# One unit of a fused transformer layer: VectorE's attention products move behind its FFN relu

## The reference

```python
q, k, v = tokens @ Wq + bq, tokens @ Wk + bk, tokens @ Wv + bv     # 16 heads of 64
S = einsum('bthd,buhd->btuh', q, k) - dist_scale * |t - u|          # a few (u, head) masked
P = softmax(S / sqrt(64), axis=u)
x = layernorm(tokens + einsum('btuh,buhd->bthd', P, v) @ Wo + bo)
z = layernorm(relu(x @ W1 + b1) @ W2 + b2 + x)                      # W1: 1024 -> 4096
```

## Time and profile before

| | us |
|---|---|
| median of 3 runs (1418.12 to 1552.58) | 1418.31 |
| the profiled execution, as timed | 1416.82 |
| its span on the slowest core, core 1 | 1415.0 |
| spans of the 8 cores | 1403.4 to 1415.0 |
| PE busy | 1288.8 (91%) |
| ACT busy | 836.9 (59%) |
| DVE busy | 788.6 (56%) |
| ACT L819, 512 exponentials | 521.6 |
| DVE L825, 512 products | 352.2 |
| ACT L1058, 176 relus of the FFN | 98.6 |
| DVE L859, 64 products with reciprocals | 44.1 |

### The profile page before, as it was taken

One profiled execution on the slowest core, in us unless ns is written; L12 is line 12 of the kernel. 1 busy time (PEld: TensorE's weight loads), 2 busy tenths in 40 slices (PEclk: granted clock), 3 DMA queues, 4 the chain that ended last, 5 costly groups with the idle time before them and its releaser, 6 DMA issues.

```text
span 1415.0 us, 20648 instructions; the slowest of 8 cores (1403.4 to 1415.0 us)
## 1 busy us (share of the span) xinstructions
PE 1288.8 (91%) x6612; PEld 618.1 (44%) x6612; DVE 788.6 (56%) x1279; ACT 836.9 (59%) x1177; POOL 37.7 (3%) x67
## 2 busy tenths in 40 slices
PE   3889899999889999999899999989999999889995
PEld 2444344444334644444355444444544444445443
DVE  5865045455468544369584443885834438773146
ACT  4755477777655756767567567674665766613122
POOL 1010100000000000000000000000000000000000
PEclk9999999999999999999999999999999999999999
DMA  9957699999943412216634222165431222677435
GB/s 230 242 162 169 110 123 122 135 120 117 120 142 106 150 58 99 94 49 176 209 103 141 93 94 84 53 186 192 131 123 64 100 91 68 173 244 216 157 89 173
DMA packets 116223, 187.65 MB, mean 133 GB/s; under 512 B 55934, under 2 KB 93828, under 8 KB 105224
## 3 DMA queue, kind: packets, MB, share of 16 engines
q1 hardware_dynamic: 87688, 156.77, 35.8%
q0 software_dynamic: 28416, 29.41, 17.9%
HBM read 178.86 MB, written 45.09 MB: 158 GB/s over the span
## 4 chain that ended last, share of the span: by engine, by line
PE 75%; DVE 9%; ACT 6%; issue 6%; DMA 3%; SPq 0%; DVEq 0%; ACTq 0%
PE PS L243 75%; ACT EB L819 2%; DVE AT L859 1%; DMA HT<-SG 1%; DVE sm L224 1%; DVE EB L825 1%; DMA VV<-x 1%; DVE sm L226 1%; ACT RT L855 1%; ACT RT L853 1%; ACT RT L856 1%; ACT H L1058 1%; DVE Y L1162 0%; DVE Y L1025 0%; DMA RG<-wcS 0%
## 5 line engine op out<-in xcount | busy, mean ns | idle before, releaser
L819 ACT ACTIVATE EB<-PS 128x1024 bf16<-128x1024 f32 x512 | 521.6, 1023 | 316.8 <-PE PS L243 312.0
L825 DVE TENSOR_TENSOR EB<-EB,DP 128x1024 bf16<-128x1024 bf16 x512 | 352.2, 690 | 415.1 <-ACT EB L819 413.2
L243 PE MATMUL PS<-RG,H 128*128 128x512 bf16 x1280 | 313.5, 383 | 29.9 <-DVE H L1114 8.6
L243 PE MATMUL PS<-EB,VV 128*128 128x512 bf16 x1024 | 307.6, 382 | 13.0 <-DVE AT L859 9.4
L243 PE MATMUL PS<-QP,KT 128*128 128x512 bf16 x1024 | 307.6, 382 | 4.5 <-ACT EB L819 2.8
L243 PE MATMUL PS<-HT,RG 128*128 128x256 bf16 (+2 forms) x1696 | 285.6, 314 | 24.5 <-ACT H L1058 11.7
L243 PEld LDWEIGHTS PS<-HT,RG 128*128 128x128 bf16 x1696 | 164.2, 99 | 133.2 <-issue 31.0
L243 PEld LDWEIGHTS PS<-RG,H 128*128 128x128 bf16 x1280 | 124.6, 99 | 187.2 <-issue 45.1
L243 PEld LDWEIGHTS PS<-QP,KT 128*128 128x128 bf16 x1024 | 100.2, 98 | 129.1 <-issue 11.7
L243 PEld LDWEIGHTS PS<-EB,VV 128*128 128x128 bf16 x1024 | 97.3, 98 | 128.1 <-issue 36.1
L1058 ACT ACTIVATE H<-PS,sm 128x256 bf16<-128x256 f32 (+1 forms) x176 | 98.6, 570 | 75.3 <-PE PS L243 75.2
(11 more groups left out here) (126 smaller groups left out, 809.3 us busy)
## 6 DMA issues: line engine op xcount, KB each, us to landing
RG<-wcW SPq DMA_DIRECT2D x64, 1024.0 KB, 5.4
RG<-wcWo SPq DMA_DIRECT2D x8, 1024.0 KB, 10.8
wcW<-W1a POOLq DMA_DIRECT2D x8, 1024.0 KB, 20.0
wcW<-W2a POOLq DMA_DIRECT2D x8, 1024.0 KB, 19.1
Y<-x1sp SPq DMA_DIRECT2D x16, 512.0 KB, 5.7
RG<-wcS SPq DMA_DIRECT2D x8, 1024.0 KB, 5.7
out<-Y SPq DMA_DIRECT2D x16, 512.0 KB, 3.2
XT<-x1sp SPq DMA_DIRECT2D x12, 512.0 KB, 4.1
```

The costliest lines, as they stand in the source:

```text
L243: return s.on("tensor", lambda e: e.matmul(out, lhsT, rhs, start=first, stop=last, skip_group_check=True), wait=wait, inc=inc)
L819: te = s.on("scalar", lambda e: e.activation(eb, po, AF.Exp, bias=-12.0, scale=1.0), wait=[tm, self.e_free[k], self.tok_consts])
L825: self.tok_p[k] = s.on("vector", lambda e: e.tensor_tensor(eb3, eb3, dp, ALU.mult), wait=[te, self.tok_dp])
```

## The change

The two L859 products leave the end of `unit_pv` and become a step of their own, `unit_at`. It is called in the following round, behind that round's `unit_scores` and fills and ahead of its `unit_pv`. The record ("at", tb) moves with them. In rounds with n % 16 == 2 the FFN's relu is made by VectorE as add and maximum; in all others ScalarE makes it as before. The second product of the FFN now waits for the last relu of either engine.

```diff
@@ unit_pv: after the exponential L856
-        for hh, ps in ((0, a), (1, b)):
+        self.late_at = tb, p, t
+
+    def unit_at(self, s):
+        if self.late_at is None:
+            return
+        tb, p, t = self.late_at
+        self.late_at = None
+        RT = self.RT
+        for hh, ps in ((0, self.bank(4)), (1, self.bank(5))):
             lo = 64 * hh
             tv = s.on("vector", lambda e, lo=lo, ps=ps: e.tensor_tensor(
                 self.AT[lo:lo + 64, 512 * p:512 * p + 512], ps[lo:lo + 64, :], RT[lo:lo + 64, :], ALU.mult),
@@ post_fill
-            th = None
+            ths = {}
...
-                th = s.on("scalar", lambda e, g=g, ps=ps, hf=hf: e.activation(
-                    hf, ps, AF.Relu, bias=self.b1c[:, g:g + 1], scale=1.0),
-                    wait=[tm, self.tok_cols, tdown])
+                if self.lagging and self.now % 16 == 2:
+                    th = s.on("vector", lambda e, g=g, ps=ps, hf=hf: e.tensor_scalar(
+                        hf, ps, self.b1c[:, g:g + 1], 0.0, ALU.add, ALU.max),
+                        wait=[tm, self.tok_cols, tdown])
+                else:
+                    th = s.on("scalar", lambda e, g=g, ps=ps, hf=hf: e.activation(
+                        hf, ps, AF.Relu, bias=self.b1c[:, g:g + 1], scale=1.0),
+                        wait=[tm, self.tok_cols, tdown])
                 self.bank_free[bk] = th
+                ths[th[0]] = th
...
-                                 wait=([tw] if g % 8 == 0 else []) + ([self.bank_free[bk], th] if g == 0 else []),
+                                 wait=([tw] if g % 8 == 0 else []) + ([self.bank_free[bk]] + list(ths.values()) if g == 0 else []),
@@ phase_b: in each round, behind scores and fills
+                self.unit_at(s)
                 if n >= 2:
                     self.unit_pv(s, n - 2)
...
         self.unit_pv(s, n - 2)
         self.unit_pv(s, n - 1)
+        self.unit_at(s)
```

## The result

The changed kernel takes 1514.4 and 1515.3 us against 1418 before: ratio 1.069, 95% interval 1.067 to 1.071. Executions in which the cores of one die ran at a lower clock (1646.7 and 1713.5 us here, 1552.6 us before) are left out on both sides. That is 97 us slower; forecast were 1508 us and a range of 1472 to 1532.

A forecast was written before the change was run, and what follows sets the result against it. TensorE bounds the kernel, by time without issuing or at a lower clock. 1416.8 us plus 67 of waits and 23 of clock gave 1507, with the median's 1.5 about 1508; range 1472 to 1532.

The forecast's parts named there:

- The place of L825: VectorE's queue: L825 ahead of the products waits for its exponential; L859 starts 1.63 us later, 2.32 to 2.34 with an L1085.
- No cover: Unit 178: fills ended at 523.11, before the opening matmul, so nothing hides the products' delay of 1.63 us or more.
- The relu: Unit 162: VectorE's relu stands behind L825, 0.9 us later than ScalarE's; the opening matmul comes 3.2 us later.
- The counts: Units 146, 274, 402: Wo fills start a round later, FFN fills drop out; 9.9 us, plus 0.9 at three other units.
- Units 242 and 370: A row stage's activation stands ahead of the exponential: about 4.1 us if it stays, 2.3 if it slips; 3.2 each taken.
- Units 98, 258, 386 and 114: Units 98, 258, 386, whose stall ends on another eviction, lose 1.7 us together; unit 114 loses 0.
- The clock: TensorE: half of 19 stalls bring a fall, 15 us, four long ones cost 8; sum 23 us, bounds 5 and 42.
- The strict reading: TensorE: the clock falls in every one of the 19 stalls, 1.6 us each, forecast about 1522 us; rival's chance 0.12.
- The clock holds: Rival: same wait, but TensorE's clock holds in stalls under 2.9 us, 1490 us or somewhat less; chance 0.20.
- the wait is smaller: Rival: slipped steps absorbed, evictions seldom land in these units; 52 us or less, no falls, 1450 to 1472; chance 0.09.
- No change: Rival: few relus go to VectorE and fills hide L859's delay, under 2%; chance 0.04.
- faster: Rival: VectorE's relu frees PE's bank sooner, taking 15 of 19.4 us of relu waits off, 1403 us; chance 0.02.

The follow-up runs named there:

- experiment 6: The changed kernel, VectorE's relus included, but in rounds with n % 16 == 2 (n from 18) L825 stands behind the products: 1439.2 us, ratio 1.014.
- experiment 4: The changed kernel with 2 to 22 idle matmuls between fills and opening matmul in 31 rounds, read by nobody: 1483.5 us, ratio 1.047.
- experiment 3: experiment 1 with the record that the products are done counted in the old round: 1474.3 us, ratio 1.040.
- experiment 1: The changed kernel without its VectorE relu, so only the products move and ScalarE makes every relu: 1490.1 us, ratio 1.051.
- experiment 7: The kernel before, but in nine rounds with FFN relus the first relus go to VectorE ahead of the products, L825 behind them: 1411.1 us, ratio 0.9945.
- experiment 5: experiment 1 with the products directly behind the next round's scores, behind L825 but ahead of the fills' evictions: 1479.8 us, ratio 1.042.
- run 178: Not a run of its own: the words "that run" mean experiment 1, and 178 is a unit of the attention phase in it.

## Why the prediction was right

**The place of L825.** Right, and the cause: experiment 6 takes back 75 us by it alone. The term of +1.63 for a unit without a VectorE eviction measured 1.51 (units 50 and 82, where the clock held). With an L1085 it was to be 2.34 and measured 2.11 in unit 178 and 2.32 in unit 322; but 1.45 in 226 and 354, 1.8 to 1.9 in 306 and 482. The ten units together cost 19 us in experiment 4 in place of 23.4. Instructions of VectorE follow each other about 0.1 us closer than their durations say (543.86, 544.47, 545.07), which the sum didn't use.

**No cover.** Right: experiment 4 fills the stalls with up to 22 matmuls, ten in unit 178, and there the opening matmul comes no later.

**The relu.** Its 0.9 us of lateness measured 0.93 in unit 162, its price 0.48 us for 256 columns and 0.74 for 512, as taken. The three 256-column units were to cost 3.2, 3.2 and 2.7 us. Unit 290 cost 2.95 in experiment 4, where the clock held; 162 and 418 cost 4.4 each there, with one fall in each. In the changed kernel they cost 6.0, 5.2 and 4.3.

**The counts.** Right in place and size: experiment 3 gives 15.9 us for the three units, their clock falls and the block starts, by the sum 10.8 and about 6 for the clock.

**Units 242 and 370.** Here I took the middle between "the row stage stays" and "it slips". It stayed: 3.9 us each in experiment 4 in place of 3.2, and 6.4 each with the clock in the changed kernel. One of the ten units counted with an eviction, 450, had none and cost 1.1. Units 98, 258, 386 and 114, put at 1.7 together, came out 2.1 us faster than before in experiment 4. Such misses cancelled: 67 us by the sum, 67 us in experiment 4 over the kernel before. That they agree to the microsecond is luck: the ten units were 4 us too dear and these four 4 too dear, while 242 and 370 were 1.4 too cheap, 162, 290 and 418 2.6 too cheap, and the few falls left in experiment 4 (31 us at the lower level, 24 before) are in it too.

**The clock.** Taken at 23 us within 5 and 42, measured at 31 by experiment 4. The price of one fall, about 1.6 us, was right: unit 34 costs 1.51 us without one and 3.15 with one, unit 178 costs 2.11 without one and 3.79 with one (experiment 1), unit 194 costs 2.32 and 3.57. That half of the 2.6 us stalls bring a fall was about right: in twelve units with a single stall of 2.3 to 2.6 us (34, 50, 66, 82; 178, 194, 226, 306, 322, 354, 434, 482) the lower level shows in 42 of 96 cases over the eight cores, and in none of 96 in experiment 4. The term that was too small is that of the units with two stalls or a long one: 162, 242, 290 and 370 and the three empty ones have 6 to 7 us at the lower level on nearly every core, two falls; the sum had only four long ones, at 2 us each, not much over one fall. In the whole phase the core at the page's head has 126 us at the lower level, 24 before. Half of the 102 more, 51 us, would be the price had TensorE been dense all along; it was 31.

The Trainium skill (TensorE: Matmul & The Clock Gate, the part on the HAM clock gate) says that activity lifts the throttle. Experiment 4 agrees: activity alone, with no useful result, holds the clock at 0.98 to 0.99. The strict reading that the prediction made of it, a fall in every stall, is refuted here: 54 of the 96 stalls left the clock alone.

**The rivals.** "The clock holds" fell with the falls just counted, "the wait is smaller" with experiment 3. "No change" and "faster" fell as they were argued, on L825's wait for its exponential. The mechanism of "faster" was sound under the condition named there, that L825 is out of the relu's way: experiment 7 makes it so, and gains 7.8 us where 15 had been put down for all relu waits.

## What to carry to other kernels

In a queue that is worked off in order, an operation's cost is set by what stands ahead of it and what that waits for. Before moving an operation behind another, read in the trace when the other's operand arrives; VectorE had been free for 2.5 us, but only for work whose input was ready. A step that is counted in rounds moves more than itself: look for preconditions that were met in the very round in which they were asked. And stalls of some 2.5 us in a TensorE-bound stretch are dearer than they look, since a third to a half of them (32 of 96 in experiment 1, 42 of 96 in the changed kernel) also halved the clock for a while.

## What the runs showed of the hardware

A single stall of 2.3 to 2.6 us in otherwise dense work lowered TensorE's clock in 42 of 96 cases, stalls of 4 to 5 us in units 130, 146, 242, 274, 370 and 402 in all 48, and ones of 1.75 us in unit 450 in none of 8. In experiment 5 nine units of blocks 1 to 3 had single stalls of 1.75 to 2.03 us, and none of those 72 cases brought a fall. Matmuls that nobody reads, put into the stalls, held the clock and gave 31 us. I had not expected that the same stall, at the same place of the program, brings a fall on one core and not on its neighbour.

The cases are not independent draws. In experiment 1 the cores that fell in units 34 and 66 held in 50 and 82, and the others the other way round, on all eight cores. In blocks 1 to 3 of that run 178 and 306 fell on every core and the six other units of the twelve on none; in the changed kernel 178 fell on none of the eight, 226 and 354 on all. So a share of falls holds for a whole run, and says little of one place.
